# Graph attention on one core: the normalised tokens are turned by two transposing DMAs a step instead of by TensorE

## The reference

```python
h = jnp.maximum(_layernorm(x, axis=-1), 0.0)
q, k, v = (_split_heads(h @ W + b) for W, b in ((Wq, bq), (Wk, bk), (Wv, bv)))
scores = jnp.einsum('bhqd,bhkd->bhqk', q, k) / sqrt(32)
scores = jnp.where(adj > 0, scores + beta * adj, -9e15)
out = x + jnp.einsum('bhqk,bhkd->bhqd', softmax(scores), v)
```

## Time and profile before

| | |
|---|---|
| median of 3 runs | 1080.31 us |
| the profiled execution | 1079.27 us, span 1077.4 us |
| TensorE (PE) busy | 1020.8 us, 95% |
| VectorE (DVE) busy | 967.6 us, 90% |
| ScalarE (ACT) busy | 884.5 us, 82% |
| GpSimd (POOL) busy | 567.5 us, 53% |
| mean granted TensorE clock | 0.992 |
| DMA | 129 GB/s; the SP queue's packets take 47.1% of 16 engines' span |

### The profile page before, as it was taken

The page is one execution under the profiler, slowest core; times in us unless marked ns, Lnnn a source line. Parts: engine busy times, 40 slices in busy tenths (PEclk is TensorE's granted clock), DMA queues, the critical chain, the costliest instruction groups (busy, mean ns, idle before and its releaser), DMA issues. The chain is left out here.

```text
span 1077.4 us, 33776 instructions
## 1 busy us (share of the span) xinstructions
PE 1020.8 (95%) x10959; PEld 709.7 (66%) x10959; DVE 967.6 (90%) x4343; ACT 884.5 (82%) x2343; POOL 567.5 (53%) x756
## 2 busy tenths in 40 slices
PE   3899999999999999999999999999999999999986
PEld 2466676666666666666666667666666666667664
DVE  6579998999899999999999999999999999999897
ACT  3378888888888888888888888888888888888887
POOL 3645655445665445565444565544565544565431
PEclk9899999999999999999999999999999999999997
DMA  5454445554444554444554444554444554444441
GB/s 156 108 132 129 113 127 139 158 134 127 107 133 132 157 138 129 111 129 136 150 140 132 111 130 129 150 145 134 130 107 132 144 150 134 130 104 135 117 116 41
DMA packets 91038, 138.79 MB, mean 129 GB/s; under 512 B 15600, under 2 KB 66288, under 8 KB 90864
## 3 DMA queue, kind: packets, MB, share of 16 engines
q1 hardware_dynamic: 90336, 135.85, 47.1%
q10 hardware_dynamic: 528, 0.79, 0.2%
HBM read 35.91 MB, written 25.17 MB: 57 GB/s over the span
## 5 line engine op out<-in xcount | busy, mean ns | idle before, releaser
L523 ACT ACTIVATE probs<-biased,neg_max 128x128 f32<-128x128 f32 x1536 | 490.5, 390 | 146.9 <-DVE neg_max L638 115.5
L437 PE MATMUL ps_p<-hT,w 128*128 128x512 f16 x1728 | 423.5, 382 | 23.9 <-DVE hT L609 18.7
L638 DVE CUSTOM_DVE_ANT_0 biased<-ps_s,mask 128x128 f32<-128x128 f32 x1536 | 353.5, 286 | 75.8 <-PE ps_s L458 74.5
L336 POOL TENSOR_TENSOR on<-on,xb 128x384 f32<-128x384 f32 x128 | 128.0, 1000 | 380.9 <-DVE on L659 380.1
L437 PEld LDWEIGHTS ps_p<-hT,w 128*128 128x128 f16 x1728 | 167.5, 98 | 175.7 <-DVE hT L609 26.1
L644 DVE TENSOR_TENSOR pT<-ps_t,pT 128x512 f16<-128x512 f32 x384 | 263.3, 686 | 0.9 <-ACT pT L548 0.9
L466 PE MATMUL ps_t<-ident,probs 128*128 128x128 f32 x1536 | 245.4, 283 | 0.1
L548 ACT ACTIVATE pT<-ps_t 128x512 f16<-128x512 f32 x384 | 220.5, 574 | 1.0 <-PE ps_t L466 1.0
L437 PE MATMUL ps_p<-w,hT 128*128 128x384 f16 x1152 | 207.6, 326 | 0.0
L458 PEld LDWEIGHTS ps_s<-k_st,q_st 96*128 96x128 f16 x1536 | 117.5, 97 | 81.3 <-DVE neg_max L638 6.9
L481 PE MATMUL ps_o<-v,pT 128*128 128x33 f16 x1536 | 157.1, 179 | 8.9 <-DVE pT L644 5.2
(11 more groups left out here) (62 smaller groups left out, 1016.8 us busy)
## 6 DMA issues: line engine op xcount, KB each, us to landing
q_st<-qT SPq DMA_DIRECT2D x384, 96.0 KB, 2.2
k_st<-kT SPq DMA_DIRECT2D x384, 96.0 KB, 2.2
out<-on SPq DMA_DIRECT2D x128, 192.0 KB, 2.1
xs<-in_x SPq DMA_DIRECT2D x31, 768.0 KB, 5.0
adjs<-in_adj SPq DMA_DIRECT2D x32, 256.0 KB, 5.0
xs<-in_x ACTq DMA_DIRECT2D x1, 768.0 KB, 7.1
k_st<-in_L_gnn_Wq SPq DMA_DIRECT2D x1, 576.0 KB, 5.6
k_st<-in_L_gnn_Wk SPq DMA_DIRECT2D x1, 576.0 KB, 9.3
```

The source lines that it names most:

```text
L336: pool.tensor_tensor(on[:, j % 2, :], on[:, j % 2, :], xb[:, par, j, :], ALU.add).then_inc(added, 1)
L437: mm = pe.matmul(dst, stationary, moving, start=m == 0, stop=m == MMS - 1)
L523: act.activation(probs[:, odd, i, :], biased[:, odd, i, :], ACT.Exp, bias=neg_max[:, odd, i:i + 1], scale=-1.0).then_inc(exp_done, 1)
L638: dve.tensor_tensor_reduce(out=biased[:, odd, i, :], in0=ps_s[:, i * N:(i + 1) * N], in1=mask[:, gp, v // CH, :], scale=-1.0, scalar=3.0e3 ...
```

## The change

ScalarE now normalises and clips the tokens (`normalise`, four ACTIVATEs a step, two in slot 3 and two in slot 4) straight from `xs` into `hn`, with a scale and a shift for each token; POOL computes the shift (`rstd_of`) and splits `hn` into a high and a low fp16 part, `h_parts` (`split_tokens`). SyncE turns each part with one transposing DMA (`turn_tokens`, 128x12x128 fp16) into `hT`, whose layout is now graph by block by token. The turn units are gone from TensorE, with `turn_high` and `turn_low`; ten units are left to share the three banks, in the order q, k, v. The first step's tokens are still turned on TensorE (`turn_first`). TensorE waits once a step, at the first projection matmul, for both transposing DMAs (`hT_in`).

```diff
-    UNITS = ([("q", c) for c in range(CH)] + [(kind, c) for c in range(CH) for kind in ("k", "turn")]
-             + [("v", j) for j in range(G)])
+    UNITS = ([("q", c) for c in range(CH)] + [("k", c) for c in range(CH)] + [("v", j) for j in range(G)])
...
+            def turn_tokens(s, par):
+                wait(sp, proj_done, NB * (s - 1))
+                for a, split in enumerate((h_high, h_low)):
+                    sp.wait_ge(split, G * s)
+                    sp.nop(nofuse=True)
+                    sp.dma_start_transpose(hT[:, par, a].rearrange("p j c t -> p (j c) t"),
+                                           h_parts[:, a].rearrange("p j d -> p (j d)")).then_inc(hT_in, 16)
...
+                if 0 <= s <= STEPS - 2:
+                    turn_tokens(s + 1, 1 - par)
                 if attend:
                     store(s - 1, 0)
                 if proj:
                     spread(s, par, "k")
...
+                pool.tensor_tensor(shift[:], neg_mean[:], rstd[:], ALU.mult).then_inc(shift_done, 1)
+
+            def split_tokens(s, j):
+                pool.wait_ge(normed, G * s + j + 1)
+                wait(pool, hT_in, 32 * (s - 1))
                 pool.nop(nofuse=True)
-                for j in range(G):
-                    pool.tensor_scalar(hn[:, j, :], xs[:, par, j, :], neg_mean[:, j:j + 1], rstd[:, j:j + 1],
-                                       ALU.add, ALU.mult).then_inc(normed, 1)
+                pool.tensor_copy(h_parts[:, 0, j], hn[:, j]).then_inc(h_high, 1)
+                pool.wait_ge(h_high, G * (s - 1) + j + 1)
+                pool.tensor_tensor(h_parts[:, 1, j], hn[:, j], h_parts[:, 0, j], ALU.subtract).then_inc(h_low, 1)
...
+                    if o == 0 and m == 0 and s >= 1:
+                        pe.wait_ge(hT_in, 32 * s)
...
+            def normalise(s, par, j):
+
+                act.wait_ge(shift_done, s + 1)
+                if s == 1:
+                    act.wait_ge(h_turned, CH)
+                wait(act, h_low, G * (s - 2) + j + 1)
+                act.activation(hn[:, j, :], xs[:, par, j, :], ACT.Relu, bias=shift[:, j:j + 1],
+                               scale=rstd[:, j:j + 1]).then_inc(normed, 1)
...
+                    if ahead and u in (3, 4):
+                        for j in range(2 * (u - 3), 2 * (u - 2)):
+                            normalise(s + 1, 1 - par, j)
```

More of the change, by code:

```diff
@@ L59, in graph_attention_kernel @@
     for o, (kind, n) in enumerate(UNITS):
[L60 to L63, removed]
+        ATOMS += [(o, m, D if kind == "v" else TOK) for m in range(MMS)]
     TOTAL = sum(a[2] for a in ATOMS)
@@ L75, in graph_attention_kernel, with bank_of @@
     PB = 3
-    BANK = [[(o + par) % PB for o in range(NB)] for par in range(2)]
-    ENDED = [[o for o, a, b in PIECES[u] if UNITS[o][0] == "turn" or b == MMS] for u in range(SLOTS)]
+    def bank_of(s, o):
+        return (NB * s + o) % PB
+    ENDED = [[o for o, a, b in PIECES[u] if b == MMS] for u in range(SLOTS)]
     x_v = x.rearrange("(s j) t d -> s t j d", j=G)
@@ L352, in step @@
                     add_bias(s, par, 2)
+                if 0 <= s <= STEPS - 2:
+                    for j in range(G):
+                        split_tokens(s + 1, j)
                 if older:
@@ L390, in _, with bank_free, turn_first @@
         def _(pe):
-            def bank_free(s, par, o):
+            def bank_free(s, o):
                 if s == 0 and o < PB:
-                    pe.wait_ge(h_low, o + 1)
+                    pe.wait_ge(first_low, o + 1)
                     return
[L396 to L409, removed]
-                else:
-                    wait(pe, qk_low, QK * before + QK_AT[last] + 1)
-            def turn(s, bank, c):
-                pe.wait_ge(normed, G * (s + 1))
+                before, last = divmod(NB * s + o - PB, NB)
+                kind, n = UNITS[last]
+                if kind == "v":
+                    pe.wait_ge(v_copied, G * before + n + 1)
+                else:
+                    pe.wait_ge(qk_low, QK * before + last + 1)
+            def turn_first(bank, c):
+                pe.wait_ge(normed, G)
                 for j in range(G):
@@ L422, in project @@
                 kind, n = UNITS[o]
-                bank = ps_p[BANK[par][o]]
+                bank = ps_p[bank_of(s, o)]
                 if first == 0:
-                    bank_free(s, par, o)
+                    bank_free(s, o)
                 if first == 0 and n == 0 and s == 0:
@@ L439, in project @@
                     mm.then_inc(proj_done, 1)
[L441 to L448, removed]
             def scores(n, g, gp, v, odd):
@@ L496, in step @@
                     if proj:
-                        piece(s, par, u, ahead)
+                        for o, first, end in PIECES[u]:
+                            project(s, par, o, first, end)
             pe.wait_ge(consts_set, 3)
@@ L505, in _ @@
             for c in range(CH):
-                turn(0, ps_h[c], c)
+                turn_first(ps_h[c], c)
             for n in range(2):
@@ L524, in exps, with first_high_part @@
                                    bias=neg_max[:, odd, i:i + 1], scale=-1.0).then_inc(exp_done, 1)
[L526 to L530, removed]
+            def first_high_part(bank, c):
+                act.wait_ge(h_turned, c + 1)
+                act.activation(hT[:, 0, 0, :, c, :], bank[:].rearrange("p (j t) -> p j t", t=N),
+                               ACT.Copy).then_inc(first_high, 1)
+            def normalise(s, par, j):
[5 more added lines that the diff above has]
+                               scale=rstd[:, j:j + 1]).then_inc(normed, 1)
             def high_part(s, par, o):
                 kind, n = UNITS[o]
-                bank = ps_p[BANK[par][o]]
-                act.wait_ge(proj_done, NP * s + PROJ.index((kind, n)) + 1)
+                bank = ps_p[bank_of(s, o)]
+                act.wait_ge(proj_done, NB * s + o + 1)
                 if kind == "v":
@@ L560, in step @@
                         for o in ENDED[u]:
[L561 to L564, removed]
+                            high_part(s, par, o)
+                    if ahead and u in (3, 4):
+                        for j in range(2 * (u - 3), 2 * (u - 2)):
+                            normalise(s + 1, 1 - par, j)
             for n in range(3):
@@ L568, in _ @@
                 act.activation(w_sq[:, n], w_raw[:, :, W_COLS[n]], ACT.Square).then_inc(w_squared, 1)
+            for j in range(G):
+                normalise(0, 0, j)
             def weights_high(n, ready, count):
@@ L604, in mask_linked, with first_low_part @@
                                          op0=ALU.mult, op1=ALU.add).then_inc(mask_done, 1)
[L606 to L611, removed]
+            def first_low_part(bank, c):
+                dve.wait_ge(first_high, c + 1)
+                dve.tensor_tensor(hT[:, 0, 1, :, c, :], bank[:].rearrange("p (j t) -> p j t", t=N),
+                                  hT[:, 0, 0, :, c, :], ALU.subtract).then_inc(first_low, 1)
             def low_part(s, par, o):
                 kind, n = UNITS[o]
-                bank = ps_p[BANK[par][o]]
-                dve.wait_ge(qk_high, QK * s + QK_AT[o] + 1)
+                bank = ps_p[bank_of(s, o)]
+                dve.wait_ge(qk_high, QK * s + o + 1)
                 dst, b = (qT, 0) if kind == "q" else (kT, 1)
@@ L672, in step @@
                     if u >= 1 and proj:
-                        low_parts(s, par, u - 1, ahead)
-                    if u == 0 and s >= 1:
-                        low_parts(s - 1, 1 - par, SLOTS - 1, s <= STEPS - 1)
+                        low_parts(s, par, u - 1)
                     if ended:
```

35 lines of the change are left out of this document (16 added, 19 removed).

## The result

The changed kernel takes 1098.47 us (median of 4 runs, 1097.34 to 1101.66) against 1080.16 for the kernel before: a ratio of 1.0178, 95% interval 1.0166 to 1.0191. It is 1.8% slower, where 4.5% faster was forecast. The time lies inside the wide range, but the direction was wrong. It is rival C's direction, though the queue is held for less than C's 6.2 us: X lies in B's interval.

What follows compares the result with a forecast made beforehand. TensorE was taken to bound the kernel, with SyncE's queue almost as long. 1079.3 - 40.9 (turn units) - 18.7 (waits for hT) + 6 (ScalarE) + 5 (step 0) = 1030.7, against the median 1032 us; range 1012 to 1330.

Steps and rivals of the forecast that it cites:

- rival C: SyncE's queue: X over 6.2 us makes it the bound; 1209 us at 10 us, 1435 at 17.3; chance 0.33.
- X: Time two transposing DMAs hold SyncE's queue and DMA engines per step, without landing: taken 3 to 4 us, free to 4.3.
- B: SyncE's queue takes back part of the gain: X between 4.3 and 6.2 us, 1066 us at 5.4; chance 0.14.
- What goes: TensorE loses 93 turn units, 40.9 us, and the wait for hT, 18.7 us: together 59.6 us, 1.9 a step.
- Spread q's pace: SyncE's queue: pricing the transposes at 96 KB in 0.68 us, 8 times, gives X of 5.4 us.
- upper bound of 17.3 us: DMA engines: 3072 pieces of 256 bytes at 90 ns each over 16 engines give X of 17.3 us.
- The rest of SyncE's chain: SyncE from slot 3 to next slot 3, everything besides X: 25.9 us, in a step of 30.2 us.
- ScalarE's crowd: Normalising operations in slots 3 and 4 delay exponentials for TensorE: 0.2 us a step taken, at most 0.75; +6 us.
- GpSimd at nothing: GpSimd's added splits cost nothing: 20.6 us busy of 30, with 3.7 us in hand before SyncE needs its sums.
- Step 0: First step, no attention to hide anything: spread k, already 1.2 us late, is pushed by X; 5 us once.
- A: The forecast itself: X at most 4.3 us on SyncE's queue, time 1032 us; chance 0.44.
- D: TensorE waits on: ScalarE's crowd at 0.75 us a step (1049), bank waits elsewhere (1051), or both (1068); chance 0.09.

Runs made afterwards that it cites:

- best version: Changed kernel with third x buffer, x load at step head, adj load after spread k, moments and deviations a step early, normalising in slots 0, 1, 4, 5: 1028.87 us.
- loads moved: Changed kernel with a third x buffer, the load of x issued at the head of the step and the load of adj after spread k: 1056.86 us.
- doubled best version: The best version with each transposing DMA followed by a second one of the same source into a spare tile: 1147.44 us.

## Why the prediction was wrong

**What goes: right.** The best version takes the units away and lands at 1028.9 us with a 30.28 us step. TensorE is busy 43.2 us less than before (977.6 for 1020.8), and the 18.7 us of waits for a bank are not in its list.

**The step that failed is the term that decides, X: "I take 3 to 4 us, nearest to the load of x".** In the changed kernel X is 5.77 us. The transposes by themselves do cost 3.5 (loads moved), inside what I took; but the number was for transfers that find the engines free. The prediction placed them right behind the load of adj and reckoned the store and the two loads at their issue time alone, 1.9 us, though the earlier trace rows already gave the load of x 5.0 us to landing. Spread q's pace, which gave 5.4, was nearer only by accident: it knows nothing of the loads either. At the other end, the upper bound of 17.3 us took 90 ns for each small piece; from the queue's share of the engines' time, 62.2% of 1054.8 us with the loads moved and 47.1% of 1077.4 us before, the 97216 added packets take an estimated 25 ns each.

**The rest of SyncE's chain was 1.0 us short** (32.71 - 5.77 = 26.9 for 25.9). The store behind the transposes, with the gaps beside it, takes 1.3 us and not 0.5, and spread k 8.2 us in the mean (7.5 to 9.0), where I had read 7.6 from one step. Against it 0.3 us are less from the end of spread k to the next spread q, 7.4 for 7.7: I had counted the whole 2.2 us of landing behind the issuing, of which it overlaps some 0.6. Put together the chain is 32.7 us, 2.5 over the 30.2 of the forecast: 1.5 from X and 1.0 from the rest. At 31 steps that is 46 and 31 us; with ScalarE's allowance of 6 us taken off, since this chain covers it, 1032 - 6 + 77 = 1103 us, 5 more than measured.

Moving the loads gave back 41.6 us, close to the 46 that X above 4.3 costs by the formula. That closeness is in part luck: the chain was 1.0 us longer than in the formula, and what took over as the bound was 31.3 us and not 30.2.

**ScalarE's crowd was under-sized too: "I take 0.2 us a step", at most 0.75.** With the loads moved TensorE waits for it 28.4 us, 0.95 us a step. The mechanism and the place were as described; the price of one operation was read from a copy out of PSUM (0.47 us), and the new one reads SBUF with a scale and shift of its own:

```profile
L535 ACT ACTIVATE hn<-xs,shift,rstd 128x384 f32<-128x384 f32 x128 | 82.7, 697 | 5.1 <-POOL shift L320 5.1
```

It takes 0.70 us, half as much again. In the changed kernel this shows as 12.1 us only, because the other chain is longer and hides the rest. It is not what made the change slower: with the loads moved and the crowd in place the kernel takes 1056.9 us and is faster than before. It is what keeps that kernel 25 us above the forecast.

**GpSimd at nothing: right as the change stands**, and its cover is as thin as was said: spreading the normalising operations alone cost 60 us.

**Step 0:** the first step grew from 24.5 to 29.0 us between loads of x, 4.5 us for the 5 taken.

**The rivals:** A was wrong. X at 5.77 lies in B's interval, whose formula gives 1032 + 46 = 1078 us, no loss; the time came out on C's side because the rest of the chain was short as well, which no rival had. D's mechanism was real but ran beside the chain and not on top of it: adding B at 5.8 and D's upper bound, 1032 + 46 + 17 = 1095, comes near 1098 only by chance. The 1309 ns for a block on the Trainium skill's page "VectorE: DVE Perf Modes" (section "The three transpose paths"), by which I estimated 31 us, is not the rate of blocks in one large transfer here: 24 blocks hold the queue for 3.5 us. The 261 GB/s of the Trainium skill's page "DMA: Bandwidth & Descriptors" (section "Latency and other measured facts"), which it gives for a non-contiguous middle dimension, are nearer: 786 KB in 3.5 us would be 225 GB/s, and four transposes in a row in the doubled best version, 7.6 us, make it 208. Both are estimates from the time on the queue.

## What to carry to other kernels

Price a transfer together with what is on the same engines just ahead of it: take a load's landing time, not its issue time, for whatever transposing DMA stands behind it and in front of something that a chain waits for, and put bulk loads where nothing urgent follows. When work moves off the bounding engine, work out every other chain with the new work on it, and add up each by means over many steps and not by one: here SyncE's chain ended 2.7 us early, the step was to shrink by 1.9, and with the 3.5 us of the old wait for the store the new work had 4.3 us, of which the means took another 1.0. The longest chain sets the step; the prices of two chains are not added, but when the longer one is cured the other is what remains. Where work lands on an engine matters by slot: the same four operations cost 0.95 us a step in two adjacent slots of ScalarE; one at a time that wait is gone, but 0.4 us a step come back through the engines that wait for the last of them, and with the loads in place the same edit costs 60 us.

## What the runs showed of the hardware

- Two transposing DMAs of 384 KB (128 x 1536 fp16, SBUF to SBUF) hold SyncE's queue for 3.5 us with no loads just ahead of them, 5.8 us behind 1 MB of loads. Two plain copies of the same size hold it for 1.2 us behind the same loads. Each transpose adds (187552 - 90336) / 62 = 1568 packets, 251 bytes each in the mean.
- The scores that need the last DMA of spread k start 1.62 to 1.74 us after the queue has issued it, in 28 of 28 steps.
- An ACTIVATE from SBUF with per-partition scale and bias, 128x384 fp32, takes 0.70 us, where a copy of the same size out of PSUM takes 0.47; two of the first kind in a row follow each other at 0.60 us.
- Gaps of 0.85 and 1.69 us in TensorE left the next matmuls at their old pace (1.67 us for seven, granted clock 1.00); one of 3.44 us was followed by a granted clock of 0.50 (1.2 GHz) for two microseconds, and 1.00 (2.4 GHz) from the fourth on.
